# A graph layer's output stage: one wait place per block on TensorE, a new order of its three parts, and table loads four windows ahead

## The reference, cut to what matters

```python
h = jnp.maximum(_layernorm(x, axis=-1), 0.0)
# messages of both directions, from h at both ends and the edge's features
agg  = segment_sum(mlp2_f(concat[h[src], h[dst], edge]), dst)
agg += segment_sum(mlp2_r(concat[h[dst], h[src], edge]), src)
node_in = concat[agg, h]                                    # 128 + 64 columns
out = x + h + (relu(node_in @ Wn1 + bn1) @ Wn2 + bn2)       # 128 hidden, 64 out
```

## Time and profile before

| | |
|---|---|
| time, median of 3 runs | 1585.3 us (1584.4 to 1585.63) |
| profiled execution | 1586.92 us, its span 1585.2 us |
| TensorE busy in the span | 1284.4 us (81%) |
| VectorE, ScalarE, GpSimd busy | 972.0, 940.2, 1094.1 us |
| output stage | its first transposes start at 1331.56 us; to the end of the span |
| granted clock of TensorE, mean | 0.855; 1.00 from 1340 to 1580 us |

### The profile page before, as it was taken

One profiled execution on the slowest core, in us unless ns is written; L12 is line 12 of the kernel. 1 busy time (PEld: TensorE's weight loads), 2 busy tenths in 40 slices (PEclk: granted clock), 3 DMA queues, 4 the chain that ended last, 5 costly groups with the idle time before them and its releaser, 6 DMA issues.

```text
span 1585.2 us, 29464 instructions
## 1 busy us (share of the span) xinstructions
PE 1284.4 (81%) x7070; PEld 975.8 (62%) x7070; DVE 972.0 (61%) x3294; ACT 940.2 (59%) x2256; POOL 1094.1 (69%) x985
## 2 busy tenths in 40 slices
PE   5889988747778887787778888777778873999998
PEld 4677777535556666565556666656656652777776
DVE  7999999636666666666666666666666650222222
ACT  4888888635555555545455555555545532777776
POOL 8889878878888888888888888888888863000000
PEclk9999999778887778778887777878887776999999
DMA  6899998535555555555555555555555545999998
GB/s 201 296 315 313 315 313 304 173 60 110 105 110 110 110 105 106 105 105 106 105 99 103 103 103 106 106 105 104 100 104 96 101 91 153 382 371 370 365 363 298
DMA packets 238986, 281.00 MB, mean 177 GB/s; under 512 B 53746, under 2 KB 155776, under 8 KB 238924
## 3 DMA queue, kind: packets, MB, share of 16 engines
q1 hardware_dynamic: 168696, 241.57, 45.7%
q0 software_dynamic: 68992, 38.59, 19.9%
q10 hardware_dynamic: 1236, 0.30, 0.1%
HBM read 162.62 MB, written 117.72 MB: 177 GB/s over the span
## 4 chain that ended last, share of the span: by engine, by line
POOL 54%; issue 24%; PE 18%; DMA 2%; DVE 1%; POOLq 1%; ACT 0%; SPq 0%; DVEq 0%
POOL table L541 30%; POOL got_even L523 13%; POOL got_odd L523 7%; PE bank L888 6%; PE bank L899 6%; POOL to_send L583 4%; PE bank L909 3%; DMA table<-to_send,scatter_at 2%; PE bank L863 1%; PE bank L837 0%; PE bank L835 0%; DVE same L996 0%; PE bank L850 0%; DMA same<-table 0%; DMA gather_begin<-in_src 0%
## 5 line engine op out<-in xcount | busy, mean ns | idle before, releaser
L541 POOL DMA_INDIRECT table<-to_send,scatter_at x392 | 622.2, 1587 | 133.0 <-issue 117.1
L863 PEld LDWEIGHTS bank<-message,same 128*128 128x128 f32 x1960 | 272.3, 224 | 41.9 <-issue 39.5
L863 PE MATMUL bank<-message,same 128*128 128x128 f32 x1960 | 293.2, 315 | 2.2 <-DVE message L1028 2.2
L656 ACT ACTIVATE nh<-nx,all_sums,all_rstd 128x64 f32<-128x64 f32 x784 | 280.1, 433 | 0.0
L523 POOL DMA_INDIRECT got_even<-in_x,gather_first x192 | 207.4, 1080 | 37.7 <-issue 37.7
L821 PE MATMUL bank<-ident,h_ends 128*128 128x128 f32 x196 | 55.0, 376 | 218.0 <-DVE h_ends L1037 218.0
L792 PE MATMUL bank<-wn_h,nturned 128*128 128x256 f32 x784 | 196.0, 393 | 31.3 <-ACT nhidden L700 26.6
L523 POOL DMA_INDIRECT got_odd<-in_x,gather_at x180 | 179.9, 999 | 54.9 <-issue 54.9
L996 DVE TENSOR_SCALAR_CACHE_REDUCE same<-others,ids 128x128 f32<-128x128 int32 (+3 forms) x392 | 190.7, 543 | 12.7 <-DVE ids L988 11.0
L792 PEld LDWEIGHTS bank<-wn_h,nturned 128*128 128x128 f32 x784 | 142.7, 192 | 67.5 <-issue 34.8
L1022 DVE TENSOR_TENSOR scatter_at<-moved,ids 128x4 int32<-128x4 f32 x98 | 15.9, 162 | 265.4 <-DMA table<-to_send,scatter_at 265.4
(11 more groups left out here) (81 smaller groups left out, 2012.9 us busy)
## 6 DMA issues: line engine op xcount, KB each, us to landing
nx<-in_x SPq DMA_DIRECT2D x194, 256.0 KB
table<-nhidden SPq DMA_DIRECT2D x97, 512.0 KB
same<-table SPq DMA_DIRECT2D x97, 512.0 KB, 5.3
others<-numbers SPq DMA_DIRECT2D x196, 128.0 KB
out_x<-nh SPq DMA_DIRECT2D x79, 256.0 KB, 4.0
nx<-out_x SPq DMA_DIRECT2D x55, 256.0 KB, 4.3
out_x<-ncentred SPq DMA_DIRECT2D x49, 256.0 KB, 4.3
table<-to_send,scatter_at POOLq DMA_INDIRECT x392
```

What stands on the lines that cost most here:

```text
L541: pool.indirect_dma_start(table, bass.IndirectOffsetOnAxis(ap=scatter_at[s][:, k:k + 1], axis=0), to_send[s][:, k, :], None, compute_op=AL ...
L656: last = act.activation(nh[s][:, g, :], nx[place][:, g, :], ACT.Relu, bias=all_sums[:, at, g:g + 1].rearrange("p a g -> p (a g)"), scale=a ...
L863: last = pe.matmul(bank[6 + s][:, k * M:(k + 1) * M], same[s][:, o, k * P:(k + 1) * P], message[s][:, o, :], start=(o == k), stop=(o == KB ...
```

## The change

On TensorE the waits are taken out of `turn_table`, `layer2_nodes` and `turn_back` and stand together at the head of a window's block, in three functions of their own. The block becomes `turn_back` of w - 2, `layer2_nodes` of w - 1, `turn_table` of w + 1, with the first `turn_table` ahead of the loop. Two waits go: that of `layer2_nodes` for the earlier bias and that of `turn_table` for the relu, which other waits of the block cover. On SyncE four tables instead of three are asked for ahead of the loop, and the body asks for w + 4 instead of w + 3.

```diff
-            for k in range(3):
+            for k in range(NRING):
                 Step(NW, 0).do(load_table, k, ring=NRING)
 
             def window(w):
-                w.do(load_table, 3, ring=NRING)
+                w.do(load_table, 4, ring=NRING)
                 w.do(store, -2, ring=NRING)
...
             def turn_table(i, s, turn, place):
-                pe.wait_ge(n_tab[place], 16 * (turn + 1))
-                if not first(i):
-                    pe.wait_ge(n_hidden[s], 2 * i)
                 for odd in range(2):
...
             def layer2_nodes(i, s):
-
-                if not first(i):
-                    pe.wait_ge(n_biased[s], i)
-                pe.wait_ge(n_hidden[s], 2 * (i + 1))
                 for c in range(0, 512, 256):
...
             def turn_back(i, s):
-
-                pe.wait_ge(n_biased[s], i + 1)
-                if not first(i):
-                    pe.wait_ge(n_out[s], i)
                 for q in range(G // 2):
...
+            def wait_biased(i, s):
+
+                pe.wait_ge(n_biased[s], i + 1)
+                if not first(i):
+                    pe.wait_ge(n_out[s], i)
+
+            def wait_hidden(i, s):
+
+                pe.wait_ge(n_hidden[s], 2 * (i + 1))
+
+            def wait_table(i, s, turn, place):
+                pe.wait_ge(n_tab[place], 16 * (turn + 1))
+
             def window(w):
-                w.do(turn_table, ring=NRING)
+
+                w.do(wait_biased, -2)
+                w.do(wait_hidden, -1)
+                w.do(wait_table, 1, ring=NRING)
                 w.do(turn_back, -2)
                 w.do(layer2_nodes, -1)
-
+                w.do(turn_table, 1, ring=NRING)
+
+            wait_table(0, 0, 0, 0)
+            turn_table(0, 0, 0, 0)
             run(pe, NW, [(4, 96, 4)], 2, window)
```

More of the change, by code:

```diff
@@ L903, in turn_back @@
             def turn_back(i, s):
+                for q in range(G // 2):
+                    last = pe.transpose(bank[6 + s][:, q * P:(q + 1) * P], nturned[s][:, q * P:(q + 1) * P], ident[:, :])
+                last.then_inc(n_back[s], 1)
+            def wait_biased(i, s):
                 pe.wait_ge(n_biased[s], i + 1)
@@ L907, in turn_back @@
                     pe.wait_ge(n_out[s], i)
-                for q in range(G // 2):
-                    last = pe.transpose(bank[6 + s][:, q * P:(q + 1) * P], nturned[s][:, q * P:(q + 1) * P], ident[:, :])
-                last.then_inc(n_back[s], 1)
+            def wait_hidden(i, s):
+                pe.wait_ge(n_hidden[s], 2 * (i + 1))
+            def wait_table(i, s, turn, place):
+                pe.wait_ge(n_tab[place], 16 * (turn + 1))
             def window(w):
-                w.do(turn_table, ring=NRING)
+                w.do(wait_biased, -2)
+                w.do(wait_hidden, -1)
+                w.do(wait_table, 1, ring=NRING)
                 w.do(turn_back, -2)
                 w.do(layer2_nodes, -1)
+                w.do(turn_table, 1, ring=NRING)
+            wait_table(0, 0, 0, 0)
+            turn_table(0, 0, 0, 0)
             run(pe, NW, [(4, 96, 4)], 2, window)
```

## The result

The changed kernel takes 1596.84 us (median of 4 runs, 1596.09 to 1597.75) against 1585.47: the ratio is 1.0072, 95% interval [1.0054, 1.0089]. It is 11.4 us slower, where +9.6 was forecast. The profiled execution has a span of 1596.0 us, 10.8 more than before.

A forecast was written before the change was run, and what follows sets the result against it. The output stage was taken as bound by the bias, turn_back, layer2_nodes circle and equally turn_table's transposes with the bias. Held waits +10.1, earlier loads -0.5: +9.6 us, forecast 1594.9 us, range 1583 to 1601.

The forecast's parts named there:

- The circle: Output stage: bias, B (turn_back), L (layer2_nodes), bias set a 2.47 us period, with T (turn_table) beside the bias.
- Waits taken out of T and L give back nothing: TensorE's turn_table and layer2_nodes: holes of 0.38 and 0.17 us a window come from changing weight tiles; gain costed at nothing.
- Rival (a): TensorE's holes around layer2_nodes were the waits' own, so 0.15 us a window closes and the kernel ends faster; chance 0.09.
- Three windows of four hold the bias wait: Ahead of turn_back, new values behind the bias wait make TensorE's sequencer hold it: three windows of four, before one.
- rival (b): Ahead of turn_back the bias wait still rides on the weight load: -1.6 us, 1583.7, no difference; chance 0.08.
- Its size: Bias end to turn_back's weights 0.23 us in three windows; turn 10.46 against 10.02, 10.1 us more over 23 turns.
- 0.14 was named as the sign: Weight loads' idle time ahead of turn_back was to grow from 0.04 to about 0.14 us on average.
- The table wait 1.6 us earlier: The table wait moves ahead of turn_back and layer2_nodes; four loads ahead cover it with 2.3 us left, before 1.2.
- Rival (d): A table comes late in the early turns and the whole block stands, 1597 us in all; chance 0.04.
- The loads alone give back part of the early excess: Loads four ahead can give back at most 1.7 us of early table waits; 0.5 us was taken.
- the DMAs were near their limit at 392 GB/s: DMA engines moved 392 GB/s in the output stage's first turns, taken as near their limit, with room later.
- rival (c): The held bias wait's delay is paid but hidden beside turn_table's transposes: 1585 us, no change; chance 0.05.

The follow-up runs named there:

- bias_last: Changed kernel, its four waits still in one place but ordered table, relu, n_out, bias: 1587.04 us against 1583.98 for the kernel before, ratio 1.002.
- bias_alone: Changed kernel with only the bias wait ahead of turn_back, the others moved to layer2_nodes and turn_table: 1582.55 us against 1584.0 before, ratio 0.9991.
- The 9.89 with no held wait: Kernel with the bias wait alone ahead of turn_back, plus ScalarE's older waits in relu_nodes and add_bias left out: 1579.97 us against 1584.0 before.
- the two half kernels: Changed kernel with layer2_nodes computing one half only, with 64 columns of weights or with 128: 1596.66 and 1578.95 us, one run each.
- the pairs kernel: Kernel with the bias wait alone ahead of turn_back, reworked to take windows in pairs on TensorE and ScalarE: 1570.7 us against 1583.98 before, ratio 0.9916.

## Why the prediction held, point by point

- *The circle.* Bias, B, L, bias as the pace, with T beside it: shown by the turns that follow the delay behind the bias. Against the changed kernel, `bias_last` has 0.34 us less of it in four windows and a turn 0.36 shorter; `bias_alone` has 0.25 less again and a turn 0.21 shorter. The 9.89 with no held wait fits but doesn't decide, because TensorE's own work comes to the same.
- *Waits taken out of T and L give back nothing.* Right: the holes at L885 and L892 are 0.38 and 0.17 us a window as before, and 0.10 and 0.05 when the tile doesn't change. Rival (a) is excluded. By the Trainium skill, "TensorEngine Tiling (Array Packing)", section "Key Properties", a change of the tiling mode drains TensorE; the two half kernels agree with it, 11.5 against 3.2 us; the transposes of L824, at the end of this document, do not show it.
- *Three windows of four hold the bias wait, one doesn't.* Right; rival (b), that it still rides on the weights, is excluded by 0.21 to 0.32 us in those three.
- *Its size.* The forecast took 0.23 us for each of the three. Two have 0.22 and 0.21. The third has 0.32, since a third value was new there, that of n_out, which I had not counted: three sequencer steps and not two. The term came out as 0.51 a turn and not 0.44. Over the 23 turns, with what the early ones give back, that is 11.4 us and not 10.1 less 0.5. The opening gives back another 0.5, which I had put at nothing, so the span grew by 10.8 us against 9.6 forecast; the medians, 11.4 us apart, add about 0.5 of run-to-run difference. That the number came so near is in part luck: the step not counted is worth 23 x 0.09 = 2.1 us, the other two delays were taken 0.03 too long together (0.7 us), and the opening goes the same way as these. The hole ahead of B grew to 0.17 us a window, where 0.14 was named as the sign.
- *The table wait 1.6 us earlier is covered with four in flight.* Right for the changed kernel: between 1340 and 1590 us no wait of B, L or T was ended by a table. Rival (d) didn't happen, but the kernel with three in flight, 0.8 us short on average, shows what it would have looked like.
- *The loads alone give back part of the early excess.* Right, 0.36 us by the turns where 0.5 was taken. The premise that the DMAs were near their limit at 392 GB/s was wrong: the pairs kernel had 413.
- *Hidden beside T*, rival (c): excluded, the late windows are longer by the full delay.

The Trainium skill, "Perfetto Trace Analysis", section "Per-engine timelines", has the sequencer wait itself in a sequencer-only instruction, while other instructions wait in a queue behind it. The steps of 0.10 us agree with that.

## What to carry to other kernels

Ask of every wait on the path what the engine's sequencer still has to do between that wait's end and the first real instruction. Where loop counts are register values, put the wait that ends last where no new value is computed behind it, best alone on its instruction. Waits that are long satisfied are not free either, if they stand behind the one that ends last: each sequencer instruction that they need there cost about 0.10 us. And a wait that moves ahead of other work needs its data earlier by all of that work: here 1.6 us, which one more load in flight paid for.

## What the runs showed of the hardware

- Sequencer instructions between a wait's end and the weights cost time on TensorE: 0.05, 0.11 to 0.13, 0.21 to 0.22 and 0.32 us for none to three. That is 0.06 to 0.08 us for the first and about 0.10 for each further one.
- The hole between 128x128 weights and matmuls with 128x64 appears even when only the first column half is used. But the transposes of the edges' features in the second stage, also with weights of 64 columns between others of 128, show next to none in the kernel before, 1.6 us over 158 loads. What sets the two apart no run here tells.

```profile
L824 PEld LDWEIGHTS bank<-ident,edge_in 128*64 128x64 f32 x158 | 23.5, 149 | 1.6
```

- A DMA rate of 392 GB/s was not the limit: the pairs kernel had 413 GB/s over 20 us in the same stage.
